# A recommender tower in float32: spreads and look-ups of the first two tiles reordered, late weights loaded earlier

## The reference, cut to what matters

```
e  = stack of 26 table rows, tbl_f[ids[:, f]]              # 512 x 26 x 32
x1 = einsum('bik,bjk,hij->bhk', e,  e, W1) + b1            # CIN layer 1, 128 maps
x2 = einsum('bik,bjk,hij->bhk', x1, e, W2) + b2            # CIN layer 2, 128 maps
z  = sum over k of concat([x1, x2], axis=1)                # 512 x 256
h  = relu(concat([z, dense_ctx]) @ W_top1 + b_top1)        # 272 -> 512
h  = relu(h @ W_top2 + b_top2)                             # 512 -> 256
y  = h @ W_top3                                            # 512 x 1
```

## Time and profile before

| what | value |
| --- | --- |
| runs of the kernel before | 164.77, 164.77, 166.09 us, median 164.77 |
| the profiled execution | 165.63 us, its span 163.9 us |
| mean granted TensorE clock | 0.969 of full speed |
| busy: PE, DVE, ACT, POOL | 94%, 67%, 52%, 43% of the span |
| chain that ended last | PE 86%, DMA 5%, ACT 5% |
| DMA | 9.07 MB |

### The profile page before, as it was taken

One profiled execution on the slowest core, in us unless ns is written; L12 is line 12 of the kernel. 1 busy time (PEld: TensorE's weight loads), 2 busy tenths in 40 slices (PEclk: granted clock), 3 DMA queues, 4 the chain that ended last, 5 costly groups with the idle time before them and its releaser, 6 DMA issues.

```text
span 163.9 us, 3319 instructions
## 1 busy us (share of the span) xinstructions
PE 154.4 (94%) x1261; PEld 146.2 (89%) x1261; DVE 109.9 (67%) x338; ACT 85.9 (52%) x229; POOL 70.7 (43%) x76
## 2 busy tenths in 40 slices
PE   6979999289999999799999999999999999999994
PEld 6969999199999989698999999989999899999993
DVE  5838899999997248799667799555787962231000
ACT  1123479907988714974444675335448644560032
POOL 2777777755394734454637354636350000000000
PEclk9999999857999999969999999999999999999999
DMA  5997110005470003100000001000000000000000
GB/s 159 363 401 285 16 18 13 12 8 178 151 265 12 11 7 118 42 8 16 8 12 14 8 9 16 4 10 18 6 14 0 4 0 0 4 0 0 4 0 1
DMA packets 4930, 9.07 MB, mean 55 GB/s; under 512 B 1617, under 2 KB 3217, under 8 KB 4914
## 3 DMA queue, kind: packets, MB, share of 16 engines
q1 hardware_dynamic: 2130, 6.25, 10.6%
q0 software_dynamic: 2176, 1.12, 4.1%
q10 hardware_dynamic: 608, 1.49, 2.5%
HBM read 8.85 MB, written 0.00 MB: 54 GB/s over the span
## 4 chain that ended last, share of the span: by engine, by line
PE 86%; DMA 5%; ACT 5%; DVE 1%; issue 1%; SPq 0%; ACTq 0%
PE bank L363 19%; PE bank L376 13%; PE bank L371 11%; PE bank L313 11%; DMA small<-in_small_dram 5%; PE bank L415 5%; PE bank L385 5%; PE bank L334 4%; PE bank L329 4%; ACT diag L553 3%; PE bank L405 3%; PE bank L408 2%; PE bank L403 2%; PE bank L340 2%; PE bank L392 2%; PE bank L423 1%
## 5 line engine op out<-in xcount | busy, mean ns | idle before, releaser
L283 POOL DMA_INDIRECT rows<-in_tbl_dram,idx x68 | 69.9, 1027 | 50.4 <-DMA rows<-in_tbl_dram,idx 31.1
L363 PE MATMUL bank<-diag,prod 128*128 128x108 f32 x256 | 33.1, 285 | 3.6 <-ACT diag L553 3.6
L363 PEld LDWEIGHTS bank<-diag,prod 128*128 128x128 f32 x256 | 31.9, 201 | 4.4 <-issue 4.1
L553 ACT ACTIVATE diag<-prod,quad 128x416 f32<-128x416 f32 (+2 forms) x48 | 22.0, 538 | 10.0 <-DVE prod L694 9.9
L526 ACT COPY t<-bank 128x432 f32<-128x432 f32 x32 | 15.0, 522 | 21.7 <-PE bank L363 21.6
L376 PEld LDWEIGHTS bank<-t,v 128*128 128x128 f32 x208 | 24.8, 192 | 1.5
L726 DVE COPY t<-bank 13x128 f32<-13x128 f32 (+2 forms) x48 | 12.6, 263 | 19.8 <-PE bank L371 19.3
L376 PE MATMUL bank<-t,v 128*128 128x128 f32 x208 | 25.1, 275 | 0.0
L678 DVE TENSOR_TENSOR w1p<-bank,chosen 128x320 f32<-128x320 f32 (+2 forms) x28 | 15.0, 536 | 12.6 <-PE bank L313 11.5
L313 PE MATMUL bank<-small,idb 128*128 128x256 f32 (+1 forms) x72 | 22.1, 414 | 1.2 <-DMA small<-in_small_dram 1.2
L371 PE MATMUL bank<-diag,prod 128*77 128x64 f32 x256 | 21.0, 236 | 0.0
(11 more groups left out here) (70 smaller groups left out, 171.8 us busy)
## 6 DMA issues: line engine op xcount, KB each, us to landing
idb<-in_idt_dram SPq DMA_DIRECT2D x4, 576.0 KB, 5.9
rows<-in_tbl_dram,idx POOLq DMA_INDIRECT x68, 2.4
wt<-in_W_top_dram SPq DMA_DIRECT2D x2, 512.0 KB, 3.7
w2t<-in_w2t_dram SPq DMA_DIRECT2D x1, 768.0 KB, 11.9
small<-in_small_dram SPq DMA_DIRECT2D x1, 672.0 KB, 8.9
w1t<-in_w1t_dram SPq DMA_DIRECT2D x1, 640.0 KB, 4.0
small<-in_small_dram SPq DMA_DIRECT2D x1, 608.0 KB, 10.3
w1p<-in_w1p_dram ACTq DMA_DIRECT2D x1, 521.0 KB, 3.8
```

The source lines that it names most:

```text
L283: pool.indirect_dma_start(rows[t][:, f, :], None, tables[f], bass.IndirectOffsetOnAxis(ap=idx[:, t, f:f + 1], axis=0)).then_inc(s_got[t][p ...
L363: mm = nc.tensor.matmul(m0[:, g % GBANK, :, 0:JW], prod[:, G, 0:P], diag[:, G, :, :], start=True, stop=True)
L553: ins = nc.scalar.activation(diag[:, :, r, f0:f1], prod[:, :, col:col + f1 - f0], ACT.Identity, scale=quad[:, r:r + 1])
```

## The change: other places for spreads, look-ups and weight loads

- BEHIND: each look-up of tile 0 stands one fold later.
- SP issues w1t, wt1, wt1c and wt2 without waiting for the steps of tile 0.
- spread(0, 2) is gone from ScalarE; VectorE copies these three fields into the diagonal of `diag` in half_b(0), and a new semaphore s_late tells TensorE. The memset of `diag` at the start covers these columns as well. spread(0, 1) stands before the last two copies of ctB, and step(0, 0) waits for all copies but these two; step(0, 1) waits for these.
- Look-ups 2 to 6 of tile 1 stand earlier in TensorE's program.
- spread(1, 1) and spread(1, 2) stand where they do in the later tiles.
- The add that makes z1w stands behind turn(1, 1) on VectorE.

```diff
-BEHIND = {1: 0, 2: 1, 3: 2, 4: 3, 5: 4, 6: 5, 7: 6}
+BEHIND = {2: 0, 3: 1, 4: 2, 5: 3, 6: 4, 7: 5, 8: 6}
...
             sp.dma_start(idb[:, 1, :], on_all(io["idt"], 1)).then_inc(s_idb[1], 16)
-            sp.wait_ge(s_m0, 1)
             sp.dma_start(w1t[:], io["w1t"]).then_inc(s_w1t, 16)
-            sp.wait_ge(s_m0, 2)
             sp.dma_start(wt1[:], io["W_top1"][0:2 * H, :].rearrange("(c p) n -> p c n", p=P)).then_inc(s_wt, 16)
             sp.dma_start(wt1c[:], io["W_top1"][2 * H:2 * H + D_CTX, :]).then_inc(s_wt, 16)
-            sp.wait_ge(s_m0, 3)
             sp.dma_start(wt2[:], io["W_top2"].rearrange("(c p) n -> p c n", p=P)).then_inc(s_wt, 16)
...
                 if s == 0:
                     pe.wait_ge(s_pa, t + 1)
-                    pe.wait_ge(s_diag, (t + 1) * len(PARTS))
                     if t == 0:
-                        pe.wait_ge(s_sf, DONE["ctB"])
+                        pe.wait_ge(s_late, 1)
+                        pe.wait_ge(s_sf, DONE["ctB"] - 2)
+                    pe.wait_ge(s_diag, (t + 1) * len(PARTS) - 1)
+                if t == 0 and s == 1:
+                    pe.wait_ge(s_sf, DONE["ctB"])
...
                 make(q)
+            look_up(1, 2)
             for q in range(HIGH, DONE["v1"]):
                 make(q)
+            look_up(1, 3)
             pe.wait_ge(s_sf, HIGH)
-            z2(0, HALF)
-            look_up(1, 2)
+            z2(0, 7)
+            look_up(1, 4)
+            look_up(1, 5)
+            z2(7, HALF)
+            look_up(1, 6)
             pe.wait_ge(s_eg, STEPS)
             for q in range(DONE["v1"], len(SETUP)):
                 make(q)
-            look_up(1, 3)
             pe.wait_ge(s_sf, DONE["v1"])
             z2_low(0, False)
-            look_up(1, 4)
             pe.wait_ge(s_sf, len(SETUP))
-            for i, (j0, j1) in enumerate(((13, 17), (17, 21), (21, FIELDS))):
-                z2(j0, j1, j1 == FIELDS)
-                if i < 2:
-                    look_up(1, 5 + i)
+            z2(HALF, FIELDS, True)
...
             spread(0, 0)
-            for q in range(FOLDS + 1, DONE["ctB"]):
+            for q in range(FOLDS + 1, DONE["ctB"] - 2):
                 take(q)
             spread(0, 1)
-            spread(0, 2)
+            for q in range(DONE["ctB"] - 2, DONE["ctB"]):
+                take(q)
             evict(0)
...
-                if more and t:
                     spread(t + 1, 1)
...
-                    spread(t + 1, 2 if t else 1)
+                    spread(t + 1, 2)
                 relu1(t)
-                if t == 0:
-                    spread(1, 2)
                 relu2(t)
...
-            link(nc.vector.memset(diag[:, :, :, ONE:JW], 0.0))
+            link(nc.vector.memset(diag[:, :, :, PARTS[2][0]:JW], 0.0))
...
+                if t == 0:
+                    for r in range(QUADS):
+                        q = slice(32 * r, 32 * r + 32)
+                        ins = nc.vector.tensor_copy(diag[q, :, r, f0:f1], prod[q, :, col:col + f1 - f0])
+                    ins.then_inc(s_late, 1)
                 dve.wait_ge(s_fac[2], t + 1)
...
                 pick(1, i)
-                if i == 1:
-                    dve.wait_ge(s_w1t, 16)
-                    nc.vector.tensor_tensor(z1w[:], w1t[:, 0, :, :], w1t[:, 1, :, :], ALU.add).then_inc(s_z1w, 1)
                 if i == 5:
                     turn(1, 0)
             turn(1, 1)
+            dve.wait_ge(s_w1t, 16)
+            nc.vector.tensor_tensor(z1w[:], w1t[:, 0, :, :], w1t[:, 1, :, :], ALU.add).then_inc(s_z1w, 1)
```

More of the change, by code:

```diff
@@ L203, in dlrm_tower @@
         s_diag = sem("s_diag")
+        s_late = sem("s_late")
         s_ident = sem("s_ident")
```

## The result

The changed kernel takes 165.41 us in the median of 20 runs, against 164.81 of 20 runs of before beside it: ratio 1.0043, 95% interval 1.0023 to 1.0064. Run once more beside later experiments it gave 165.31 against 164.85, ratio 0.9998 (0.9971 to 1.0025). The medians mislead a little: of the 20 runs of before, 12 took 164.6 to 164.9 us and seven 165.8 to 166.1, so their median stands in the lower group, while those of the change lie evenly between 164.3 and 166.0. The means of all runs are 165.28 against 165.11, and 165.20 against 165.22 the second time. So the change gains nothing; whether it loses a little (0.6 and 0.5 us by the medians, 0.2 and 0.0 by the means) isn't settled. The profiled execution took 165.17 us with a span of 163.4.

The account below looks back on a forecast made before the run. TensorE was taken as the bound, with the start of step(1, 0) deciding: 163.9 - 73.4 + 70.4 + 1.9 = 162.8 of span, + 1.73 = 164.5 us. Likely range 163.0 to 166.2, chance 0.70.

Parts of the forecast that it names:

- The hole before tile 0: TensorE's wait for ScalarE's spreads before step(0, 0) shrinks from 3.9 to some 1.6 us.
- Only look_up(1, 2) decides: TensorE reaches it at 45.2, waits for pick(1, 0)'s multiply until 50.7, and loses there what the early start won.
- The late copies: VectorE's four copies into diag, on its gapless stretch, delay the adds and pick(1, 0) by 0.8 us, 0.4 to 1.1.
- The wait for z: Layer 1's 1.10 us hole on TensorE before 67.52 closes, as z is there before the last chunk.
- Rivals A and B: A: full clock after the new hole, 162.6 us, chance 0.12; B: no new hole, 160.0 to 162.8, chance 0.05.
- keep their times: Look-ups of tile 0 stay in time, a 0.62 us fold fills part of TensorE's 1.19 us wait before 10.73.
- Weights at once: Early weight load meets POOL's gathers of tile 0 and delays turn(0, 0) by 0.3 us, 0 to 1.5.
- rival C: Queue 1's weight load holds a gather of tile 0 and shifts VectorE; slower by 1% or more, chance 0.13.
- Behind the hole: TensorE's work from look_up(1, 2) at 50.7 to step(1, 0) takes 19.7 us at full clock.
- The price c: Loss to the low clock behind the new hole: 1.9 us, between 2.75 and 1.6; ends 1.0 and 2.75.
- The comparison: Forecast 164.5 us set against 165.63 of the profiled execution of before and a median of 164.77.

Follow-up runs that it names:

- experiment 1: The change with TensorE's old order behind the steps of tile 0, look-ups 2 to 6 of tile 1 in their old places: 163.46 us, ratio 0.990 to before.
- experiment 2: The kernel before with only the look-ups of tile 1 in the new order: 162.16 us, ratio 0.9843 to before.
- experiment 5: The change with TensorE's order behind tile 0's steps, spread(1, 1), spread(1, 2) and the z1w add as before: 161.05 us, ratio 0.9746 to before.
- experiment 6: The change with w1t, wt1, wt1c and wt2 sent during the steps of tile 0, as before: 165.19 us, ratio 0.9986 to before.
- experiment 3: The change with 20 products of no use on TensorE ahead of look_up(1, 2): 163.12 us, ratio 0.9871 to before.
- 7: Early start as in experiment 5, look-ups of tile 1 earlier, but look_up(1, 2) behind L343 and the first half of z2: 160.13 us, ratio 0.969 to before.
- experiment 4: The change with the look-ups of tile 0 behind folds 1 to 7 as before: 164.66 us, ratio 0.9971 to before.

## Why the prediction went as it did

**Right, and shown.** The hole before tile 0 at 1.6 us (1.57). Only look_up(1, 2) decides: TensorE there at 45.2 (45.8), released by the multiply at 50.7 (50.44 to 50.61), so that all of the front's gain is waited out. Experiments 1, 2 and 5 show it from three sides: the early start alone gains 2.5%, the look-ups alone 1.6%, and together they gain nothing. (The moved spreads and the add of z1w are in neither half; the spreads cost 0.3 us, below.) The late copies at 0.8 us: L719 fills 28.26 to 29.19 in the chain, 0.9, and L897 starts 0.87 later than L894 did. The wait for z gone. Rivals A and B: the clock fell in each profiled execution of the change, and the hole was there in all.

**Wrong, at small cost: the look-ups of tile 0 "keep their times".** look_up(0, 0) started at 11.05 instead of 10.73, with no wait before it, right behind the third fold. TensorE's 44 products ahead of the folds had taken 7.92 us instead of 6.61, so the fold didn't find the whole hole that it was to fill. The set-up then ended 0.4 us earlier instead of 0.62, and tile 0 started at 30.76, not 30.35; the hole before look_up(1, 2) took that up. VectorE's picks and turn(0, 0) came 0.24 us later, and that does reach the release. In the second profiled execution look_up(0, 0) did wait, 0.59 us for its tables, and started at 10.96.

**Weights at once: 0.3 us taken, none shown.** The eighth gather landed 5.3 us after its issue at 13.67, at 19.0, and turn(0, 0) ran at 20.57 behind the picks. So the release came near the forecast partly by luck, with another delay, the 0.24 us above, in the place of this one. An effect of 0.1 us on the small tables isn't excluded (experiment 6). The DMA table of 15.5 to 20 us after the change:

```profile
q1 hardware_dynamic: 819, 1.55, 99.0%
q0 software_dynamic: 128, 0.07, 5.3%
```

Queue 0 does get through beside a full queue 1 here, four gathers' worth, so the Trainium skill's rule of turns ("DMA: Bandwidth & Descriptors", Queues, rings and completion order) fits this stretch better than the row of 44.5 to 47.5 that I followed, and rival C didn't come.

**Wrong: a gain forecast where there is none, by two mis-sized terms and one comparison.** I forecast 164.5, 0.3 us under before's median; the medians of the change are 0.6 and 0.5 us over before's, its means 0.2 and 0.0.
- *Behind the hole* I put 19.7 us at full clock; experiment 3 measured 20.1. Of these 0.4 us, 0.3 is layer 2 waiting: L416 starts 1.20 us behind L409 there and 0.89 in 7 (63.62 to 64.51), since relu1 stands behind spread(1, 2). I had let the moved spreads pass for nothing.
- *The price c* was 1.9. Taking 20.1 from the time between look_up(1, 2) and step(1, 0) leaves 2.2 us (profile after), 2.9 (the change again), 3.0 (experiment 4) and 1.4 (experiment 6), 2.4 in the mean of these four executions, two of them of edited kernels. The step that failed is the price taken "between the two" old losses, 2.75 and 1.6, as what "belongs to a median": they came from one execution and are no ends for it, for every execution has another slow stretch behind the same hole (c went up to 3.0), and the old hole of 3.65 us itself cost 1.6 in experiment 2.
- With both, less 0.2 for the earlier release: 164.5 + 0.4 + 0.5 - 0.2 = 165.2, against medians of 165.3 and 165.4 and means of 165.2 and 165.3.
- *The comparison*: my sum stood against the profiled execution of 165.63, which had paid nearly the dearest clock. For the change I took a middle one, for before the dear one. Against it 165.2 is a gain of 0.4; against before's median a loss of 0.4, and against before's means, 165.1 and 165.2, nothing. The sum should have been made for before with the same middle c.

**Open.** Whether the fold put before look_up(0, 0) costs the median anything, as it can in executions whose first products are slow (experiment 4; look_up(0, 0) at 10.97 there without the fold, at 10.96 to 11.05 in the change); and whether the change is a little slower than before or equal, 1.0043 or 0.9998.

## What to carry to other kernels

An engine that is started earlier only arrives earlier at the next thing that it doesn't set itself: before pricing such a gain, find the first wait behind it whose releaser is on a chain without slack, and read that time. Two reorderings that gain alone (2.5% and 1.6% here) can cancel each other when one brings the engine early to a point that the other has moved forward; keep independent work ahead of that point. Where a hole costs clock as well as time, price it for both kernels alike, not for one from a single execution.

## What was not expected of the hardware

Useless work paid: 20 products in a hole of 4.6 us made the kernel 2.2 us faster, because the granted clock stayed at 1.00 instead of falling to 0.50.

The same hole, 4.7 us, was followed by 3.0, 4.6 or 6.0 us at the low clock in different executions, which moves the whole time by over 1 us. A hole of about 1 us before layer 1's last L404 was followed by a stretch at 0.50 in before and in experiment 1, and by none in experiment 5.

POOL's gathers beside VectorE's adds took 2 to 3 us of POOL instead of 0.94, with no weights on the way; timeline of POOL and the DMA table of 42 to 51 us after the change:

```profile
42.62 2.92 POOL L281 DMA_INDIRECT rows<-in_tbl_dram,idx  x1 [0.30 <-issue]
45.84 2.02 POOL L281 DMA_INDIRECT rows<-in_tbl_dram,idx  x1 [0.30 <-issue]
48.17 2.44 POOL L281 DMA_INDIRECT rows<-in_tbl_dram,idx  x1 [0.30 <-issue]
```

```profile
q0 software_dynamic: 96, 0.05, 3.3%
```

I had counted on early weights to speed these gathers; the load wasn't what held them. That VectorE's adds did is only argued from the times at which both ran: from 52.70 on, with the adds done, a gather took 0.94 us of POOL again, and before shows the same (2.02 and 2.51 us beside the adds, 0.94 from 50.08 on).
